# Other steps for the row transposes, the bias additions and the last block's rows, and rounding in two passes, in a sliding-window attention block on eight cores

## What is computed

```
xn  = LN(x)
out = x + attention(xn) + ffn(xn)
attention: q, k, v = xn @ w_in.T, 16 heads of 64; windows of 512 rows, each query sees
           its own window and the one before, 0 <= distance <= 512, with a bias
           slope[h] * distance; softmax; p @ v; @ w_out.T
ffn:       s = max(max|xn|, 1e-6) / 127 for each row
           round(xn / s) @ weight_q.T * s * weight_scale + bias
```

## Time and profile before

| | us |
|---|---|
| median of 3 runs (lowest, highest) | 1674.83 (1672.86, 1676.15) |
| the profiled execution's own time | 1680.79 |
| its span on core 4, the slowest | 1679.2 |
| spans of the eight cores | 1666.0 to 1679.2 |
| busy, core 4: TensorE | 1600.8 |
| ScalarE | 1019.5 |
| VectorE | 944.1 |
| GpSimd | 923.0 |

### The profile page before, as it was taken

The page is one execution under the profiler, slowest core; times in us unless marked ns, Lnnn a source line. Parts: engine busy times, 40 slices in busy tenths (PEclk is TensorE's granted clock), DMA queues, the critical chain, the costliest instruction groups (busy, mean ns, idle before and its releaser), DMA issues.

```text
span 1679.2 us, 28950 instructions; the slowest of 8 cores (1666.0 to 1679.2 us)
## 1 busy us (share of the span) xinstructions
PE 1600.8 (95%) x8567; PEld 816.4 (49%) x8736; DVE 944.1 (56%) x1696; ACT 1019.5 (61%) x1513; POOL 923.0 (55%) x1114
## 2 busy tenths in 40 slices
PE   4849999999999999999999999999999999999997
PEld 2325555555544555555544455555554455555553
DVE  4535646556475655646556564655646566564443
ACT  4637666666655656666565666656665565666651
POOL 5326447464575646546465655546557564655447
PEclk9979999999999999999999999999999999999999
DMA  8874453634536344354535535344453634435332
GB/s 168 193 197 117 126 136 91 147 106 126 145 101 176 108 128 124 107 139 108 138 114 148 155 108 132 114 114 138 108 138 108 188 114 114 138 107 145 76 88 70
DMA packets 208558, 214.05 MB, mean 127 GB/s; under 512 B 139788, under 2 KB 139916, under 8 KB 207882
## 3 DMA queue, kind: packets, MB, share of 16 engines
q1 hardware_dynamic: 205528, 201.70, 43.2%
q0 software_dynamic: 2880, 10.49, 3.4%
HBM read 149.22 MB, written 37.75 MB: 111 GB/s over the span
## 4 chain that ended last, share of the span: by engine, by line
PE 83%; DMA 6%; POOL 3%; issue 3%; SPq 2%; DVE 2%; ACT 0%; POOLq 0%; DVEq 0%; another core or an unknown queue 0%; ACTq 0%
PE dn L552 57%; PE sc L687 13%; PE ob L739 7%; PE oa L739 7%; DMA wqk<-w 2%; SPq L150 2%; DMA xpre<-x 2%; DMA xnfm<-xn 2%; POOL u L638 1%; POOL xq L524 1%; DVE ofm L765 0%; DMA xres<-x 0%; POOL xpre L425 0%; DMA xqfm<-xq 0%; POOL xn L439 0%
## 5 line engine op out<-in xcount | busy, mean ns | idle before, releaser
L704 ACT ACTIVATE p<-sc 128x1024 bf16<-128x1024 f32 (+1 forms) x608 | 571.0, 953 | 268.7 <-PE sc L687 267.6
L552 PE MATMUL dn<-xnfm,wqk 128*128 128x512 bf16 x2009 | 478.4, 381 | 10.1 <-DMA xnfm<-xn 6.8
L638 POOL TENSOR_TENSOR u<-u,xres 128x256 f32<-128x256 f32 x244 | 175.9, 741 | 337.6 <-DVE u L633 337.5
L723 DVE TENSOR_TENSOR p<-p,tri_sb 128x512 bf16<-128x512 bf16 (+1 forms) x608 | 248.3, 409 | 145.5 <-ACT p L704 134.6
L552 PEld LDWEIGHTS dn<-xnfm,wqk 128*128 128x128 bf16 x2048 | 195.4, 98 | 229.0 <-issue 17.8
L524 POOL TENSOR_SCALAR xq<-xqt 128x512 bf16<-128x512 f32 x128 | 250.8, 1959 | 100.6 <-DMA xqfm<-xq 79.9
L552 PE MATMUL dn<-wq_sb,xqfm 128*128 128x512 bf16 x973 | 236.3, 381 | 8.5 <-DMA xqfm<-xq 3.9
L552 PE MATMUL dn<-wv_sb,xnfm 128*128 128x512 bf16 x999 | 239.3, 379 | 1.5
L739 PE MATMUL oa<-p,vst 128*128 128x256 bf16 (+3 forms) x892 | 218.9, 300 | 22.8 <-DVE ofm L765 22.7
L552 PE MATMUL dn<-wout_sb,ofm 128*128 128x512 bf16 x1006 | 237.0, 379 | 2.4 <-DVE ofm L765 0.8
L687 PE MATMUL sc<-qb,kb 128*128 128x256 bf16 (+3 forms) x896 | 221.6, 300 | 1.7
(11 more groups left out here) (56 smaller groups left out, 1467.9 us busy)
## 6 DMA issues: line engine op xcount, KB each, us to landing
wqk<-w2bf SPq DMA_DIRECT2D x240, 256.0 KB, 3.1
xpre<-x SPq DMA_DIRECT2D x64, 512.0 KB, 4.9
xres<-x SPq DMA_DIRECT2D x64, 512.0 KB, 4.9
out<-u SPq DMA_DIRECT2D x124, 256.0 KB, 2.3
wqk<-w POOLq DMA_DIRECT2D x16, 256.0 KB, 8.0
w2bf<-wqk SPq DMA_DIRECT2D x16, 256.0 KB, 4.4
wv_sb<-wv POOLq DMA_DIRECT2D x2, 1024.0 KB, 11.5
wq_sb<-wq POOLq DMA_DIRECT2D x1, 2048.0 KB, 12.1
```

Source lines behind the costliest of these rows:

```text
L552: tok = P.op("tensor", lambda e, k=k: e.matmul(out=dn[b][:, :], lhsT=lhs(k), rhs=rhs(k), start=(k == 0), stop=(k == n - 1)), waits=(waits ...
L638: a = P.op("gpsimd", lambda e, q=q: e.tensor_tensor(out=u[:, 256 * q:256 * q + 256], in0=u[:, 256 * q:256 * q + 256], in1=buf[:, 512 * hal ...
L704: exp_done[b] = P.op("scalar", lambda e: e.activation(out=pt, in_=st, func=AF.Exp, scale=SCALE), waits=[sc_done[b]] + p_free[b % NPB])
L723: mask_done[b] = P.op("vector", lambda e: e.tensor_tensor(out=pt, in0=pt, in1=m, op=ALU.mult), waits=[exp_done[b], c_tok])
```

## The change

The row transposes `xn_turn_dma` stand in (5,4), the step of the last Q group. Rounding takes two passes, x * 1 + MAGIC in place in `xqt` and x * 1 - MAGIC to `xq`; only the second waits for `xq`. The bias additions have a table of their own, `XB_MAKE`. In the last block tiles 0 and 1 (not 1 and 2) use the `xpre` buffers, making and turning have other steps, bias additions stand in slots 5 to 7 but for the last tile's, and the GpSimd adds of x are done on `u` after its F group instead of after the P group, so that a P group is followed by the VectorE add and the store alone.

```diff
-XN_TURN_DMA = (6, 1)
+XN_TURN_DMA = (5, 4)
@@
+XB_MAKE = {(0, 1): 0, (2, 3): 1, (4, 3): 2, (5, 2): 3}
@@
-LAST_LOAD = {(0, 1): 1, (0, 2): 2, (5, 0): 0, (6, 3): 3}
-LAST_MAKE = {(5, 1): 0, (6, 0): 1, (6, 4): 2, (7, 3): 3}
-LAST_TURN = {(6, 0): 0, (6, 4): 1, (7, 3): 2}
+LAST_LOAD = {(0, 1): 0, (0, 2): 1, (5, 0): 2, (6, 3): 3}
+LAST_MAKE = {(4, 4): 0, (5, 3): 1, (6, 4): 2, (7, 2): 3}
+LAST_TURN = {(5, 2): 0, (6, 3): 1, (7, 2): 2, (7, 4): 3}
+LAST_BIAS = {(5, 2): 0, (6, 1): 1, (7, 1): 2}
 END_BIAS = (0, 0)
-END_TURN = (0, 1)
@@ xres_of
-            if t == NT - 1 and tc in (1, 2):
-                return xpre[tc - 1], xpre_free[tc - 1], f"XP{tc - 1}"
-            i = (4 * t + (1 if t == NT - 1 and tc == 3 else tc)) % NXR
+            if t == NT - 1 and tc < 2:
+                return xpre[tc], xpre_free[tc], f"XP{tc}"
+            i = (4 * t + (tc - 2 if t == NT - 1 else tc)) % NXR
@@ xq_make
+                v = P.op("gpsimd", lambda e: e.tensor_scalar(
+                    out=xqt[:, :], in0=xqt[:, :], scalar1=1.0, scalar2=MAGIC,
+                    op0=ALU.mult, op1=ALU.add), waits=[a])
                 v = P.op("gpsimd", lambda e, cols=cols: e.tensor_scalar(
-                    out=xq[:, cols], in0=xqt[:, :], scalar1=MAGIC, scalar2=MAGIC,
-                    op0=ALU.add, op1=ALU.subtract), waits=[a] + xq_free)
+                    out=xq[:, cols], in0=xqt[:, :], scalar1=1.0, scalar2=-MAGIC,
+                    op0=ALU.mult, op1=ALU.add), waits=[v] + xq_free)
@@ group_f, evac
+                if t == NT - 1:
+                    last_adds.append((t, tc, half))
@@ new function, called by group_p and by the step loop
+        def add_rows(t, tc, half, ready):
+            _, u = u_of(t, tc, half)
+            buf, free, _ = xres_of(t, tc)
+            for q in range(2):
+                a = P.op("gpsimd", lambda e, q=q: e.tensor_tensor(
+                    out=u[:, 256 * q:256 * q + 256], in0=u[:, 256 * q:256 * q + 256],
+                    in1=buf[:, 512 * half + 256 * q:512 * half + 256 * q + 256], op=ALU.add),
+                    waits=[ready, xb_ready[(t, tc)]])
+            free[:] = [a]
+            return a
@@ group_p, evac
-                for q in range(2):
...
+                a = v if t == NT - 1 else add_rows(t, tc, half, v)
@@ step loop
-                    if t == NT and at == END_TURN:
-                        xq_turn(t - 1, 3)
@@
                         xq_make(t, make_at[at])
-                        if t < NT - 1:
-                            xq_bias(t, make_at[at])
...
                             xq_make(t - 1, XQ_MAKE[at])
-                            xq_bias(t - 1, XQ_MAKE[at])
+                        if at in XB_MAKE:
+                            xq_bias(t - 1, XB_MAKE[at])
+                    for item in [k for k in last_adds if (k[0], k[1]) in xb_ready]:
+                        last_adds.remove(item)
+                        u_ready[item] = add_rows(*item, u_ready[item])
+                    if t == NT - 1 and at in LAST_BIAS:
+                        xq_bias(t, LAST_BIAS[at])
                     if t == NT and at == END_BIAS:
-                        for tc in range(4):
-                            xq_bias(t - 1, tc)
+                        xq_bias(t - 1, 3)
```

More of the change, by code:

```diff
@@ L326, in build_nc @@
         after = []
+        last_adds = []
         def xsrc(t, tc):
@@ L628, in group_p @@
             ui, u = u_of(t, tc, half)
-            buf, free, _ = xres_of(t, tc)
             cols = slice(512 * half, 512 * half + 512)
```

## The result

The changed kernel takes 1665.47 us as a median, the kernel before 1675.49 in the same series; the ratio is 0.9925, 95% interval 0.9902 to 0.9947, so 12.6 us less (9 to 16); the medians lie 10.0 apart. The forecast was 12.1 less, in a range of 1658 to 1668.5.

A forecast was written before the change was run, and what follows sets the result against it. TensorE, busy 1600.8 of 1679.2 us, was taken as the bound, so only its idle time could be won; 7.8 + 1.5 + 1.3 + 1.5 = 12.1 us off the median 1674.83 gave 1662.7, range 1658 to 1668.5.

The forecast's parts named there:

- Transposes, 7.8: Block ends: row transposes issued straight behind the weight loads end eight `xnfm` waits; 7.8 us, bounds 6.5 and 8.5.
- The slack: End of the eighth block: transposes land near 828.5, TensorE wants them at 833.6; 5 us to spare.
- the rival of half a gain: Block ends: transposes are slowed by other transfers or otherwise held, half of 7.8 is lost, 1666.6 us; chance 0.12.
- Rounding, 0 beside TensorE: GpSimd: two multiply-add passes of 0.77 us each, a tile 5.4 us against 6.1; worth nothing in the steady blocks.
- The walk of GpSimd's queue: Last block, GpSimd's work timed from P(1,1)'s add: F(2,0) waits at most 0.4 us, F(3,0) some 3 us.
- Bias steps, 3.0 on core 4 and 1.5 on the median: Steady blocks: moved bias additions let the centring come earlier, ending VectorE waits; about 3 us on core 4, 1.5 on median.
- Last block, 1.3 before the last matmul: Last block: new order starts the first projection matmul at 1659.3, not 1660.62; 1.3 us, 2.0 if the clock holds.
- core 6's 5.14: Last block: time from F(3,0)'s start to the first projection matmul at the 1.2 GHz level, 5.14 us against core 4's 4.41.
- The last output add, 1.5: Kernel end: GpSimd's adds come ahead of the projection, so the 1.40 us add and its step leave the end; 1.5 us.
- The rule of the Trainium skill: GpSimd rounding: 4 cycles an element would make each new pass as slow as the old, about 1.7 us; the forecast sided against it.

The follow-up runs named there:

- bias back: The changed kernel with the bias additions of blocks 0 to 14 right behind the making of their tile again; ratio to the kernel before 0.9891.
- weights in (6,0): The changed kernel with block 0's two large weight loads issued in step (6,0), not (4,0); ratio to the kernel before 0.9922.
- rounding alone: The kernel before with only the rounding in two multiply-add passes; ratio to the kernel before 0.9975.
- old last block: The changed kernel with the last block's tables, buffers, bias and output adds as in the kernel before; ratio to the kernel before 0.9896.
- transposes alone: The kernel before with only the row transposes moved from (6,1) to (5,4); ratio to the kernel before 0.9936.
- bias steps alone: The kernel before with only the bias additions of blocks 0 to 14 in their new steps; ratio to the kernel before 0.9998.

## Why the prediction was right, and where not

The time, the sign and the main mechanism were right: 12.6 us less, 12.1 forecast, and the largest term was the largest. By place the sum fits too, but for the last block. The blocks before it were to give 7.8 and 1.5, together 9.3, and gave 9.4 on the mean of the cores; the last block before the last matmul was to give 1.3 and gave 3.1; the end 1.5 and 1.5. By edit it fits less well:

- **Transposes, 7.8.** Right: 8.7 alone, of which some 0.6 is other waits, so 8.1 of a range of 6.5 to 8.5. The slack was there, 6.2 us in the eighth block where 5 was worked out and never under 2.5 at a later one; the rival of half a gain is out.
- **Rounding, 0 beside TensorE.** Wrong; this is the step that failed. It is worth 5.0 alone and 5.1 within the change. The pass was priced well enough (0.77 taken, 0.65 and 0.63 measured), and the step said that the first pass no longer waits for `xq`; but it then booked nothing for it. Of the 5.0 alone 1.3 lies in the blocks before the last, 3.7 in the last, where each tile hangs on the transpose of the one before and the low clock goes with the long wait; within the change all 5.1 is in the last block. The walk of GpSimd's queue did contain the short passes, so their worth was booked under the last block.
- **Bias steps, 3.0 on core 4 and 1.5 on the median.** The waits went as argued, on core 4 all 2.7 us of idle time. But their length was a property of that core and of that execution (the mean of the eight was 1.0, and 0.4 and 0.2 in two other kernels), and either the bias or the rounding removes them. Within the change the bias steps are worth nothing that can be measured; alone they cost 1.9, for the addition that they put ahead of tile 0's transpose in the last block. The walk had such additions in the last block, but not as the price of these steps.
- **Last block, 1.3 before the last matmul.** The walk was right in kind: no wait for F(2,0), one before F(3,0), the low clock. From F(0,0)'s start to the first projection matmul it was 25.8 us on core 4 and is 23.4, a gain of 2.4; the wait was 1.99 where 3 was forecast, in part because the passes are shorter than 0.77, and the low clock took 5.62 us to the projection where core 6's 5.14 was taken. On three cores the clock did not fall at all, which the forecast had allowed for. But the cause was misread: the same quick passes in the old order do as well or 0.5 better.
- **The last output add, 1.5.** Right: 1.5 on the mean of the cores.
- The rule of the Trainium skill (GPSIMD Engine Reference, performance pitfalls: 4 cycles an element for a dependent fp32 chain) did not decide here: multiply-add is as dependent as add-add and takes a third of it. The trace's own rows decided rightly. That the old pass lies near the rule's figure is by these runs no proof of it.

So the closeness of the sum is in part luck. Rounding was too low by 5, and the two parts that were given its worth were too high by 1.5 and 1.8; before the last matmul the sum is 10.6 and the measured 12.4, and by the lengths the whole gain is 13.9, not 12.6.

## To carry to other kernels

Price an edit in each place where its instruction stands in a serial chain. The same shorter pass is worth next to nothing in the middle of the run, where GpSimd has time to spare, and counts once for every link of the chain in the last block. Before a wait is booked to one of several edits, ask whether another of them removes it too: here quick passes made both the moved bias and the new order of the last block superfluous, and moving one bias behind the critical tile gave more than either. And a place in another engine's queue is not an order in time: the weight loads that were to come behind the transposes came ahead of them until a wait was put in. An in-order DMA queue is worth reading at the places where the traces of all cores disagree: the 9 us at the end of block 0 were there.

## What the runs showed of the hardware that was not expected

- On GpSimd a pass of two operations with constants over 512 columns takes 0.63 to 0.65 us as multiply-add and 1.93 to 1.96 us as add-subtract, add-add or multiply-subtract. Why was not tried.
- Four transposing DMAs hold SyncE's queue for 5.4 us at a steady boundary and for 17.2 to 20.7 us, on all eight cores, while 2 large weight loads run; one alone held it for 9.5 to 12.0 beside them and for 1.2 to 1.3 otherwise.
- The length of a wait did not decide alone whether the 1.2 GHz level followed. Waits of 1.98 to 2.06 us before F(3,0) were followed by it on 17 of 24 cores (changed kernel, bias back, weights in (6,0)); waits of 1.1 to 2.0 before F(2,0), with attention work behind it, on none of 16 (rounding alone, old last block). At 3.2 to 3.3 us before F(2,0), with the transposes alone, it followed on three of five cores, and at 5.8 to 6.0 on all eight (bias steps alone). What of the work before and after decides was not tried.
